# The order of the first loads in a gated attention and mixture kernel on one core

## The reference

```
x = x + tanh(g_xattn[0]) * L0_attention(layernorm(x), ctx, mask)     # 16 heads of 8, masked, softmax
x = x + tanh(g_ffn[0])   * L0_moe(layernorm(x))                      # sigmoid gates, top 2 of 8 experts, gelu, shared expert
x = x + tanh(g_xattn[1]) * L1_attention(layernorm(x), ctx)           # 16 heads of 8, softmax
x = x + tanh(g_ffn[1])   * L1_mix(layernorm(x))                      # r * (relu(k)^2 @ Wv), with the row before
```

## Time and profile before

| what | us |
|---|---|
| median of three runs | 323.95 |
| the three runs | 319.15, 323.95, 324.38 |
| the profiled execution | 319.62 |
| its span, first to last instruction | 317.3 |
| mean granted PE clock of the span | 0.928 |
| busy: PE, DVE, ACT, POOL | 262.6, 203.7, 184.6, 91.3 |

### The profile page before, as it was taken

One profiled execution on the slowest core, in us unless ns is written; L12 is line 12 of the kernel. 1 busy time (PEld: TensorE's weight loads), 2 busy tenths in 40 slices (PEclk: granted clock), 3 DMA queues, 4 the chain that ended last, 5 costly groups with the idle time before them and its releaser, 6 DMA issues.

```text
span 317.3 us, 7826 instructions
## 1 busy us (share of the span) xinstructions
PE 262.6 (83%) x2904; PEld 194.2 (61%) x2904; DVE 203.7 (64%) x645; ACT 184.6 (58%) x376; POOL 91.3 (29%) x161
## 2 busy tenths in 40 slices
PE   0813979999999999887997988989898869799870
PEld 0301656677678778654574756866766758679550
DVE  2320576676677687684458356876866946997980
ACT  1411345978987886985664455177677634676330
POOL 3410052143142341301101012322613512731460
PEclk9965796999999999999999999979999975999995
DMA  8457446744443443000000251444454452000121
GB/s 221 114 172 193 130 124 174 194 141 126 122 132 108 122 119 101 6 0 2 0 2 0 80 169 25 120 126 125 126 161 115 127 156 61 6 5 2 33 66 33
DMA packets 27677, 30.45 MB, mean 96 GB/s; under 512 B 13715, under 2 KB 24820, under 8 KB 26484
## 3 DMA queue, kind: packets, MB, share of 16 engines
q1 hardware_dynamic: 20446, 27.12, 29.3%
q10 hardware_dynamic: 4188, 2.47, 3.1%
q0 software_dynamic: 3008, 0.39, 0.8%
HBM read 22.43 MB, written 7.14 MB: 93 GB/s over the span
## 4 chain that ended last, share of the span: by engine, by line
PE 59%; DVE 13%; DMA 8%; issue 6%; POOL 5%; ACT 4%; ACTq 1%; SPq 1%; DVEq 0%; POOLq 0%
PE bank L1266 9%; PE bank L1227 8%; PE bank L1201 6%; PE bank L1363 5%; PE bank L1197 4%; DMA QS<-qparts 3%; DMA QS<-nmT 3%; DVE nmx L520 3%; PE bank L1166 3%; PE bank L1293 2%; PE bank L1223 2%; PE bank L1156 2%; PE bank L1143 2%; PE bank L1311 2%; PE bank L1275 2%
## 5 line engine op out<-in xcount | busy, mean ns | idle before, releaser
L520 DVE TENSOR_REDUCE nmx<-bank 128x4 f32<-128x480 f32 x128 | 82.9, 653 | 58.4 <-PE bank L1201 57.2
L411 POOL DMA_DIRECT2D QS<-nmT x94 | 46.4, 499 | 139.5 <-ACT nmT L931 139.3
L940 ACT ACTIVATE P<-bank 120x512 f32<-120x512 f32 x128 | 75.3, 592 | 18.4 <-PE bank L1227 17.2
L1227 PE MATMUL bank<-QS,KS 75*120 75x128 bf16 x512 | 53.6, 229 | 2.6 <-DMA QS<-nmT 1.6
L1201 PE MATMUL bank<-KS,QS 72*128 72x120 bf16 x512 | 51.0, 224 | 2.6 <-issue 2.6
L1201 PEld LDWEIGHTS bank<-KS,QS 72*128 72x128 bf16 x512 | 40.2, 102 | 20.8 <-issue 10.5
L1227 PEld LDWEIGHTS bank<-QS,KS 75*120 75x120 bf16 x512 | 43.7, 139 | 10.1 <-ACT P L940 2.4
L1266 PE MATMUL bank<-P,VS 120*32 120x128 f32 x1024 | 36.2, 284 | 5.4 <-DVE cn L555 4.3
L1266 PEld LDWEIGHTS bank<-P,VS 120*32 120x32 f32 x1024 | 27.5, 113 | 9.0 <-ACT P L940 4.9
L1197 PE MATMUL bank<-MB,IDH 128*128 128x480 bf16 x64 | 25.1, 392 | 5.3 <-DMA QS<-qparts 4.0
L907 ACT ACTIVATE kp<-bank,BC 128x480 bf16<-128x480 f32 x23 | 15.1, 658 | 19.5 <-PE bank L1143 11.8
(11 more groups left out here) (138 smaller groups left out, 437.1 us busy)
## 6 DMA issues: line engine op xcount, KB each, us to landing
KS<-kparts SPq DMA_DIRECT2D x48, 180.0 KB
QS<-qparts SPq DMA_DIRECT2D x42, 192.0 KB
kparts<-kp SPq DMA_DIRECT2D x24, 120.0 KB, 3.5
qparts<-qp SPq DMA_DIRECT2D x21, 128.0 KB, 3.4
QS<-nmT POOLq DMA_DIRECT2D x94, 4.0 KB, 2.2
QS<-qparts ACTq DMA_DIRECT2D x6, 192.0 KB
X<-in_x SPq DMA_DIRECT2D x3, 256.0 KB, 14.4
out<-X SPq DMA_DIRECT2D x3, 256.0 KB, 2.3
```

The lines of the kernel that those rows point to most:

```text
L411: po.dma_start(QS[G % 2][STACK + p:STACK + p + 1, k // 2, :, (k % 2) * S:(k % 2 + 1) * S], nmT[Bi % 2][p * H:(p + 1) * H, :]).then_inc(m_l ...
L520: ins = nc.vector.tensor_reduce(nmx[Bi % 2][:, UH * r:UH * r + UH], QS_BANK[U % 3][:, 0:UH * SK].rearrange("p (h k) -> p h k", k=SK), AX.X ...
L940: nc.scalar.activation(P[Bi % 2][:, hh, :], src, ACT.Exp, scale=SCALE).then_inc(exp_done, 1)
L1227: last = mm(o[0:SK, j * S:(j + 1) * S], KS[G % 2][0:ROWS, k // 2, h, (k % 2) * SK:(k % 2 + 1) * SK], QS[G % 2][0:ROWS, k // 2, h, (k % 2) ...
```

## The change

Four edits, all of them of order:

- SP's `later_loads(0)` (one weight load, two loads of x, 256 KB each) now stands at the end of the first input loads, before `k_store(0)`.
- ACT no longer issues `first_q_load(1)`. SP issues these three loads (as `q_load(0, 1)`) after it has waited until the three loads of `first_q_load(0)` have landed.
- `k_load(0, 1)` leaves its place behind `k_load(0, 0)` and stands behind `k_store(1)`.
- For group 1 `q_store(1)` stands ahead of `k_load(1, 0)` instead of behind it.

```diff
             sp.dma_start(CT[:, GK:], ctxT[:, GK:]).then_inc(c_in2, 16)
+            sp.dma_start(WT[:, 4 * 128:W1 * 128], wts[:, 4 * 128:W1 * 128]).then_inc(w_in3, 16)
+            x_load(2)
+            x_load(3)
 
             def later_loads(i):
 
-                if i == 0:
-                    sp.dma_start(WT[:, 4 * 128:W1 * 128], wts[:, 4 * 128:W1 * 128]).then_inc(w_in3, 16)
-                    x_load(2)
-                    x_load(3)
...
             k_store(0)
             k_load(0, 0)
-            k_load(0, 1)
-            later_loads(0)
+            sp.wait_ge(q_ld[0][0], 16 * PARTS)
+            q_load(0, 1)
...
                     if p == 1:
                         k_store(G)
+                        if G == 1:
+                            k_load(0, 1)
                     if p == 2:
+                        if G == 1:
+                            q_store(G)
                         k_load(G, 0, Bi)
-                        if G != NG:
+                        if G not in (1, NG):
                             q_store(G)
...
             first_q_load(0)
-            first_q_load(1)
```

## The result

| what | before | after |
|---|---|---|
| median, measured beside each other (6 runs each) | 321.57 us | 326.93 us |
| lowest and highest of these | 318.83, 326.46 | 324.25, 329.31 |
| profiled execution, span | 319.62, 317.3 | 328.35, 326.3 |
| mean granted PE clock of the span | 0.928 | 0.896 |
| busy PE, DVE, ACT, POOL | 262.6, 203.7, 184.6, 91.3 | 273.3, 204.1, 185.1, 90.9 |

The forecast was 318.2 us with 322.0 as its upper end: the 3.6 us of gain did not come. A second comparison of the same two kernels on another chip, made later, gave 1.0009 (0.9941 to 1.0077).

What follows compares the result with a forecast made beforehand. A tight PE pipeline, started late by queued Q loads: 3.7 us saved less 0.1 takes 319.62 to 316.0. With run groups at 316.0 and 320.6, it named their middle, 318.2 us, range 313.5 to 322.0.

Steps and rivals of the forecast that it cites:

- Step 1: Before the first score: second K halves leave the queue ahead of the third Q load, saving 3.7 us (3.2 to 4.0).
- The two queues don't share: Rival before the first score: Q loads still take 10.72 us, nothing gained, 319.6 or 324 us; chance 0.05.
- Step 2: Before the first score: PE finishes its K projection by about 25.0 us, before the Q load; costs and saves nothing.
- Step 3: First input loads: three more 256 KB loads fit the 11 to 14 us hole; cost 0.1 us (0 to 0.8).
- return: Behind the K loads: issuing weights and x early takes 0.786 MB out of the queue there; no time given.
- Step 4: Ninth score: second halves land at 38.0 to 40.4 us, within PE's slack; charge 0, bound 0.4 us.
- Step 5: Group 1: Q stores go first, Q loads by 42.7 us, 17th score at 52.0; saves nothing, row loads charged nothing.
- The sum: Whole kernel: 3.7 - 0.1 = 3.6 us off 319.62, giving 316.0, the shift passing through to the end.
- rival (a): PE clock rises earlier or a low-clock stretch near 31 or 46 us shrinks: 313.1 to 314.5 us; chance 0.13.
- rival (b): Part given back by late second halves, row biases or POOL's row loads: gain only 1 to 2.5 us; chance 0.15.
- Rival (d): Slower: the second half's K load lands late and PE stalls at its ninth score, 325 to 331 us; chance 0.03.
- The test that the text itself gave: If right, the distance from first score to end of span stays unchanged at 286.2 us.

Runs made afterwards that it cites:

- late inputs: Changed kernel with the early weight load and two x loads moved behind the second Q half; mean 324.10 us, ratio 0.9944 to the kernel before.
- halves and late inputs: Kernel before with group 0's second halves loaded apart, weight and x loads behind them; 324.10 us with Q stores moved first, 319.43 without.
- halves with inputs: Changed kernel with group 1's Q stores back behind its K loads; whole-kernel ratios to the kernel before 1.0049 and 0.9962.
- cut kernels: Kernels ended after the first layer's attention, everything later left out; kernel before 156.57 and 156.76 us, changed kernel 157.22 and 156.99.
- held kernel: Changed kernel ended after the first layer's attention, group 1's first Q loads waiting until sequence 1's row-maximum loads have landed; 155.40 us.

## Why the prediction was wrong

**Step 1 (second K halves leave, 3.7 us): the mechanism was right.** With late inputs the third Q load took 6.02 us in place of 10.72, and the first score came 4.4 us earlier (26.70 against 31.11). That is above the 4.0 that was the high bound, but some of it is chance: with the old first loads the third Q load took 9.78 to 11.40 us in seven profiled executions, with halves and late inputs 6.02 to 6.46 in three, and the means of the first score are 4.0 us apart (30.8 and 26.8). "The two queues don't share" fell with it.

**Step 2 (PE is ready): right.** The copy of xnT stands at 21.45 (21.0 predicted), the K correction is done at 25.41 (24.83 + 0.58; 25.0 predicted), and PE then waited 3.30 us for the Q load.

**Step 3 (early inputs, 0.1 us, 0 to 0.8): mis-sized.** The first score came at 28.71 and not at 27.4, 2.0 us behind the kernel with late inputs; over all profiled executions the early inputs cost 1.1 us there (27.9 against 26.8). The row biases did what was feared, mildly: V at 16.29 after 0.80 us of waiting, at the low clock and so 1.99 us long, and the third Q load is issued at 20.76, 0.4 us later than before. What the step said nothing of is SP's own queue: "What SP's own queue holds for the first products is issued ahead of the new loads" is true, but the K stores come behind them. From the issue of the K stores to that of the K loads it was 2.93 us before (13.78 to 16.71) and 2.92 us with late inputs (14.10 to 17.02), and 3.72 us in after (14.21 to 17.93); in all executions it was 2.92 to 2.94 without early inputs (eight) and 3.55 to 4.65 with them (twelve), 1.1 us more on the mean, the size of the whole cost. The x loads took 9.7 us to land by the page, so they did not fit the hole of 11 to 14 us. The "return" that the step named is real and was not priced: with the inputs behind the second Q half the ninth score waited 1.4 to 3.4 us for its K half.

**Step 4 (second halves in time, 0): right.** The ninth score stands at 39.94 with no wait on KS. It was due at 38.7; the later first score accounts for that. It holds only with step 3's early inputs.

**Step 5: this is the step that failed.** "Now the stores go at 40.86 - 3.7 = 37.2 at the latest, ... and the Q loads 5.5 us later, at 42.7, at the latest ... No PE wait stood there before ..., so it saves nothing by itself" came near enough: the stores went 0.8 us later than "at the latest" (38.02), since the shift was smaller, and the Q loads at 41.71, since these stores took 3.7 us and not 5.5. The next sentence was not: "POOL's row loads (L411) share the DMA engines with either batch and I charge nothing." The step looked at who needs the K and Q loads, and not at what SP sends once nothing holds it. Before, the K loads were all issued by 40.82 (38.44 + 2.38) and the Q loads, which wait for the stores behind them, left at 46.41: 5.6 us apart, with the next weights behind them. In after the gap is 0.1 us (41.61 to 41.71) and all that follows on SP moves ahead too. When POOL issues its 12 KB at 44.33, SP's queue holds 1.0 MB by the DMA records: 0.06 MB of the K loads, all 0.59 of the Q loads and 0.39 of weights. Before the row loads have landed, 0.36 MB of the next K loads (issued from 46.67) have moved too, in all 1.4 MB against 0.8 in before, and the row loads come through in 7.5 to 8.6 us in place of about 5. Price, by runs on one chip: 3.2 ± 0.4 us alone and 4.2 ± 0.8 in the changed kernel, where the step had nothing. That moving the stores costs this time is shown. That the full queue is what delays the row loads is argued from the order of the issues and from the kernel in which the Q loads and the weights were held (2.6 us, no wait); which of the two counts is open.

**The sum.** The first-layer gain of halves with inputs, 4.0 ± 0.5 us in the cut kernels, is close to the 3.6 of the sum, but in part by luck: the first score comes 2.9 us earlier on the mean (30.8 and 27.9), not 3.6, and on the third chip the profiled execution had also lost the low-clock stretch between 36 and 62 us (1.00 against 0.85), which is rival (a). With the failed step the gain becomes 0. The sum's "From the first score on nothing but engines ends the waits, so I let the shift go through to the end" fell there as well: of 2.5 us at the 13th maximum nothing was left at the 17th. The place of the loss was in rival (b), "POOL's row loads late", with a price of up to 2.6 us and 0.15; the price was larger. Rival (d), the slower one, had the wrong load: no wait on KS came in after.

**From there to the end.** The test that the text itself gave, 286.2 us from first score to end, came out at 297.6 (326.3 - 28.7). Of these 11.4 us, 3.4 arise before 60 us (2.4 ahead to 0.96 behind), none from there to 210, and 8.0 behind 210. Another execution of after lost 2.0 us in the first stretch and not 3.4 (2.8 ahead at the 13th maximum, 0.8 ahead at the 21st), so a single profile does not give the price. "The kernel's own runs fall in two groups ... 4.6 us apart" read a pattern into three runs: 103 runs of before spread from 317.2 to 333.2 around 323.45. The profiled execution of before, 319.62, was thus 3.8 us under its kernel's mean, and that of after, 328.35, 4.0 us over its own. A difference of two single profiles holds both of these. That the first measurement came out at 326.93 us, above the range, is thus mostly a matter of the stretch far behind the change. That the forecast gain is absent over all 18 runs of the kernel too (324.35 against 323.45) is what the failed step explains.

## What to carry to other kernels

A store that stands between two batches of loads, and looks like a delay, may be what keeps them, and all that follows on the queue, apart: before moving it, look at which small transfer of another queue is issued behind what now leaves early, and who waits for that. Price a small DMA by what is queued when it is issued, not by its usual landing time. Where a kernel's own runs scatter by 16 us, cut it behind the changed stretch: there 4 us stood out from 6 runs, while 12 runs of the whole kernel did not show them.

## What the runs showed of the hardware

- A row-maximum load of 4 KB, 2.2 us at the median of the page, was 7.37 us on its way with 1.0 MB waiting on another engine's queue. Between 44 and 53 us the DMA share was 0.61 in after against 0.46 before, so the engines had room on the mean and yet the small load was late. In the held kernel, with 0.02 MB moved on SP's queue meanwhile, none of the three took over 1.7 us. The Trainium skill, "DMA: Bandwidth & Descriptors", "Queues, rings and completion order", says that a completion's increment is written only after every earlier write of that DMA engine, across its queues. That would let a load of a few bytes wait for the bulk on the busy engines alone. The traces agree, but no run here tells it from plain sharing.
- On one hardware queue, stores issued behind 0.79 MB of input loads made the load that waits for them later: 3.55 to 4.65 us from the issue of the stores to that of the load in twelve executions, against 2.92 to 2.94 in eight without these inputs ahead.
- One program on one core ran at a mean granted PE clock of 0.910 or 0.939 in two executions, with spans of 319.8 and 316.5 us; over all kernels the profiled clock went from 0.894 (span 328.4) to 0.949 (314.0). In 97 runs of before the longer ones are those with the lower mean clock (correlation -0.70), so the clock goes with about half of the variance of the times; the rest is not explained.
